# A gated cross-attention and mixture-of-experts layer on one core: SyncE's queue reordered, weights in two pairs of buffers, list scatters two per tile step, small tiles gathered four ahead

## The reference

```
x = x + tanh(g_xattn) * attention(layernorm(x), ctx, ctx)      # 16 heads of 16
x = x + tanh(g_ffn) * moe(layernorm(x))

def moe(xt):                                   # 4096 tokens, 8 experts, top 2
    logits = xt @ Wr + br
    gate = softmax of the two largest logits, 0 elsewhere
    h = relu(xt @ W1[e] + b1[e])               # 256 -> 1024, for each expert e
    y = h @ W2[e] + b2[e]                      # 1024 -> 256
    return sum over e of gate[e] * y
```

## Time and profile before

| | us |
|---|---|
| median of 3 runs | 882.1 (879.96 to 883.54) |
| profiled execution | 884.82 |
| its span, first to last instruction | 883.1 |
| PE busy | 753.8 |
| DVE busy | 612.7 |
| POOL busy | 438.3 |
| ACT busy | 407.7 |

### The profile page before, as it was taken

One profiled execution on the slowest core, in us unless ns is written; L12 is line 12 of the kernel. 1 busy time (PEld: TensorE's weight loads), 2 busy tenths in 40 slices (PEclk: granted clock), 3 DMA queues, 4 the chain that ended last, 5 costly groups with the idle time before them and its releaser, 6 DMA issues.

```text
span 883.1 us, 22095 instructions
## 1 busy us (share of the span) xinstructions
PE 753.8 (85%) x6602; PEld 503.6 (57%) x6603; DVE 612.7 (69%) x1279; ACT 407.7 (46%) x784; POOL 438.3 (50%) x439
## 2 busy tenths in 40 slices
PE   3489988888888989875799789999999999999765
PEld 2145555545555555432567567767777777776543
DVE  5567899999797989974457767666666666666333
ACT  2046767776676767755233223333333333333220
POOL 5112433555555565436654745555555555554322
PEclk9579999999999999987799999999999999999788
DMA  4334655666565656544312233222222232223111
GB/s 131 109 106 120 190 167 177 185 180 171 161 168 159 182 169 179 150 111 131 91 25 38 31 45 46 47 48 48 48 48 48 48 48 48 48 42 49 26 20 23
DMA packets 96292, 85.15 MB, mean 96 GB/s; under 512 B 21702, under 2 KB 85516, under 8 KB 96108
## 3 DMA queue, kind: packets, MB, share of 16 engines
q1 hardware_dynamic: 80268, 65.72, 26.6%
q0 software_dynamic: 15680, 18.69, 13.6%
q10 hardware_dynamic: 288, 0.00, 0.0%
HBM read 53.61 MB, written 30.62 MB: 95 GB/s over the span
## 4 chain that ended last, share of the span: by engine, by line
PE 29%; DMA 26%; DVE 18%; issue 16%; POOL 5%; ACT 3%; SPq 1%; DVEq 1%; POOLq 1%; ACTq 0%
DMA out_dram<-yb,dest_idx 20%; DVE negmax L1081 6%; PE banks L1756 5%; PE banks L1658 4%; PE banks L1577 3%; DMA xg<-xn_rows,gather_idx 3%; PE banks L1554 3%; PE banks L1742 2%; PE banks L1744 2%; PE banks L1743 2%; ACT probs L882 2%; PE banks L1646 2%; DVE stats L1005 2%; POOL xg L688 2%; PE banks L1625 2%
## 5 line engine op out<-in xcount | busy, mean ns | idle before, releaser
L954 ACT ACTIVATE hid<-banks,b_col 128x256 f32<-128x256 f32 (+1 forms) x312 | 124.1, 451 | 238.7 <-PE banks L1744 128.1
L1756 PE MATMUL banks<-wall,hh 128*128 x568 | 210.1, 389 | 4.3 <-DVE yb L1495 4.1
L745 POOL DMA_INDIRECT out_dram<-yb,dest_idx x71 | 123.7, 1743 | 169.0 <-DMA out_dram<-yb,dest_idx 81.2
L1742 PE MATMUL banks<-xh,wall 128*128 128x256 f16 (+1 forms) x624 | 167.9, 272 | 15.7 <-DVE xl L1432 14.4
L1081 DVE TENSOR_REDUCE negmax<-banks 128x4 f32<-128x1024 f32 x128 | 155.8, 1217 | 27.8 <-PE banks L1625 27.2
L1743 PE MATMUL banks<-xl,wall 128*128 128x256 f16 (+1 forms) x624 | 167.8, 272 | 0.0
L1744 PE MATMUL banks<-xh,wall 128*128 128x256 f16 (+1 forms) x624 | 167.7, 272 | 0.0
L882 ACT ACTIVATE probs<-banks 128x1024 f32<-128x1024 f32 x128 | 131.1, 1024 | 67.8 <-PE banks L1646 67.3
L1756 PE MATMUL banks<-wall,hl 128*128 x568 | 147.4, 279 | 0.0
L1658 PE MATMUL banks<-probs,vaug 128*32 128x256 f32 x1024 | 84.0, 400 | 28.0 <-ACT probs L882 17.5
L688 POOL DMA_INDIRECT xg<-xn_rows,gather_idx x71 | 86.9, 1224 | 37.7 <-issue 21.2
(11 more groups left out here) (206 smaller groups left out, 1201.7 us busy)
## 6 DMA issues: line engine op xcount, KB each, us to landing
wst<-in_L_ffn_W SPq DMA_DIRECT2D x30, 512.0 KB, 5.1
k_parts<-kparts SPq DMA_DIRECT2D x48, 128.0 KB, 3.4
ks<-k_parts SPq DMA_DIRECT2D x64, 96.0 KB, 2.2
q_parts<-qparts SPq DMA_DIRECT2D x48, 128.0 KB, 2.0
qs<-q_parts SPq DMA_DIRECT2D x64, 96.0 KB
xin<-in_x SPq DMA_DIRECT2D x16, 256.0 KB, 5.4
cin<-in_ctx SPq DMA_DIRECT2D x16, 256.0 KB, 6.9
xres<-in_x SPq DMA_DIRECT2D x16, 256.0 KB, 4.8
```

Source lines behind the costliest of these rows:

```text
L745: nc.gpsimd.indirect_dma_start(out_rows, bass.IndirectOffsetOnAxis(dest_idx[par][:, s:s + 1], 0), yb[par][:, s, :], None, compute_op=ALU.a ...
L954: ins = nc.scalar.activation(hid[half][:, c % (HC // 2), 0:subs(j) * P], banks[:, b, c % 2 * TS:c % 2 * TS + subs(j) * P], ACT.Relu, bias= ...
L1742: nc.tensor.matmul(dst, hi, xh[par][:, m, 0:rows], start=(m == 0), stop=False)
L1756: ins = nc.tensor.matmul(dst, h_[:, c, s * P:(s + 1) * P], w_, start=(c == 0 and k == 0), stop=(c == HC - 1 and k == 1))
```

## The change

- SP's queue: x and context are loaded three batches ahead, behind the loads of q's first half; the weights come first in a body; xres is issued one body earlier; the second halves of ks and qs are loaded at the end of the body before; output rows and normalized rows are issued apart. At the start both stores of parts precede all reloads, and x of batch 2 is loaded at once.
- Weight halves go by turns to raw and wst, four buffers; raw gets its own place in SBUF, and xh and xl lie over it. The late halves move forward by some places.
- PE computes k of batch 1 before the first scores. Tiles 0 and 1 are gathered at the end of POOL's body 15. After the last body, the turn of batch 15 stands first; the ranks of group 6 go to step 0, its places and entries to DVE's step 0.
- POOL sends groups 6 and 7 in steps 1 to 4 and 6 to 9, two sends each, behind the gather.
- Small tiles: each half of xg has its own semaphore and holds one tile; steps 30 and 31 gather two small tiles each, later ones tile j + 4. y of small tiles goes to banks 6 and 7 by turns, and DVE makes xl, and the first half of the hidden layer, before the result.
- 14 tile steps are written out at first, and the attention loop is one lap shorter.

```diff
+at["raw"] = A[0]
+raw = [sb(f"raw{i}", [P, M * H // 2], F32, A) for i in range(2)]
...
-LEAD, PEELED, TILE_LEAD = 4, 6, 8
+LEAD, PEELED, TILE_LEAD, TABLES_AT = 4, 6, 14, 7
...
+def half_of(j):
+    return (j - BIGS) // 2 % 2
+def y_bank(j, par, s):
+    return 6 + (s if subs(j) == SUB else par)
...
+stage = [raw[0], raw[1], wst[0], wst[1]] * 2
...
+arrival = [raw, wst]
...
+    load_x(2, 1, 0)
...
-        for h in range(2):
+    for h in range(2):
+        for name in "kq":
             load_part(0, 0, name, h)
...
+        if i < 4:
+            hold(sp, stage_free[i % 2], 2 * W_KEPT + i // 2)
+        elif i >= 4:
+            hold(sp, late_lo, i - 3)
...
-        if turns:
-            load_x(m + 2, t + 1, par)
-        if maxima and within(m, 1, NB):
-            load_part(m, par, "k", 1)
-            load_part(m, par, "q", 1)
         if attention:
             max_row(m - 1, 1 - par, 1)
-        if post:
-            residual(m - 2)
+        if weights:
+            for w in range(2):
+                e = t - 1
+                wait(sp, stage_free[w], 2 * (t - 1) + par)
...
+                sp.dma_start(stage_view(arrival[par][w], w), src).then_inc(w_full[par][w], 16)
+        if isinstance(m, int) and m == NB - 2:
+            late_load(0)
+            late_load(1)
         if isinstance(m, int) and m == NB - 1:
-            late_load(2)
...
+            late_load(4)
+            late_load(5)
...
-        if post:
-            results(m - 2)
-        if weights:
...
+        if within(m, 0, NB - 4):
+            load_x(m + 3, t, 1 - par)
...
-            late_load(4)
-            late_load(5)
+            hold(sp, table_ready, 2)
+            hold(sp, list_sent, 16 * 2 * PAIR * EARLY_PAIRS)
+            for j in range(2):
+                slot_load(j)
             late_load(6)
             late_load(7)
+        if post:
+            result_rows(m - 2)
+        if within(m, 1, NB):
+            residual(m - 1)
+        if ahead:
+            load_part(m + 1, 1 - par, "k", 1)
+            load_part(m + 1, 1 - par, "q", 1)
+        if isinstance(m, int) and m == NB:
+            for j in range(2, 6):
+                slot_load(j)
+        if post:
+            norm_rows(m - 2)
+        if isinstance(m, int) and m == NB - 2:
+            late_load(2)
+            late_load(3)
...
+    def gather_small(j, par):
+        h, turn = half_of(j), (j - BIGS) // 4
+        if turn == 0:
+            hold(pool, xg_full[par], 16 * SUB * (BIGS // 2))
+            hold(pool, gT_done, BIGS - 1 + par)
+        else:
+            hold(pool, xg_half[par][h], 16 * turn)
+            hold(pool, gT_done, j - 3)
+        hold(pool, slots_full[par], 16 * (j // 2 + 1))
...
+        nc.gpsimd.indirect_dma_start(xg[par][:, h, :], None, xn2_d,
+                                     bass.IndirectOffsetOnAxis(gather_idx[par][:, h:h + 1], 0)).then_inc(xg_half[par][h], 16)
...
-        last = isinstance(m, int) and m == NB
-        if last:
+        if sending and par == 0:
+            paced(3, 3)
+        if post:
+            norm2(m - 2)
+        if isinstance(m, int) and m == NB - 1:
             hold(pool, av_mm, 8 * (NB - 1))
             hold(pool, xn2_stored, 16 * EARLY_PAIRS * 2)
             gather(0, 0, 0)
-        elif sending and par == 0:
-            paced(3, 3)
-        if post:
-            norm2(m - 2)
-        if last:
             gather(1, 0, 1)
-            for n in range(3, 6):
-                send_entry(t - 3, n)
-        elif sending and par == 0:
+        if sending and par == 0:
             paced(4, 5)
...
     residual(NB - 1)
-    tokens(NB // 2 - 2)
     gather(2, 1, 0)
     norm2(NB - 1)
     gather(3, 1, 1)
-    enlist(NB // 2 - 2, 0)
-    enlist(NB // 2 - 2, 1)
-    tokens(NB // 2 - 1)
+    tokens(NB // 2 - 2)
...
+        fixed = isinstance(j, int)
+        if not fixed or 2 <= j < BIGS - 2:
             gather(j + 2, t + 1, i)
-        if there(j, -2) and subs(j - 2 if isinstance(j, int) else j) == SUB:
+        elif j >= BIGS - 2:
+            ahead = (2 * j - BIGS + 4, 2 * j - BIGS + 5) if j < BIGS else (j + 4,)
+            for x_ in ahead:
+                if x_ < NT:
+                    gather_small(x_, x_ % 2)
+        if fixed and 1 <= j < 5:
+            send_entry(NB // 2 - 2, 2 * (j - 1))
+            send_entry(NB // 2 - 2, 2 * (j - 1) + 1)
+        if fixed and j == 5:
+            tokens(NB // 2 - 1)
+        if fixed and 6 <= j < 10:
+            send_entry(NB // 2 - 1, 2 * (j - 6))
+            send_entry(NB // 2 - 1, 2 * (j - 6) + 1)
+        if fixed and j == EARLY - 3:
+            hold(pool, xn2_stored, 16 * NB)
+        if there(j, -2) and subs(j - 2 if fixed else j) == SUB:
             scatter(j - 2, i, 1, t - 1)
         if there(j, -1):
             scatter(j - 1, 1 - i, 0, t + (i - 1) // 2)
-        if isinstance(j, int) and j in (3, 4):
-            enlist(NB // 2 - 1, j - 3)
-        if isinstance(j, int) and j == TILE_LEAD - 1:
...
+        if isinstance(j, int) and j == 0:
+            act.wait_ge(late_lo, 5)
...
-        late_at_step = {NB - 1: {0: 0, 1: 1, 6: 2, 7: 3}, NB: {2: 4, 3: 5, 4: 6, 5: 7}}.get(m, {}) if isinstance(m, int) else {}
+        late_at_step = {NB - 1: {0: 0, 1: 1, 3: 2, 4: 3, 6: 4, 7: 5}, NB: {0: 6, 1: 7}}.get(m, {}) if isinstance(m, int) else {}
...
+                if isinstance(m, int) and m == NB:
+                    high_x(0, 0)
...
-        late_at_step = {NB - 1: {1: 0, 2: 1, 7: 2}, NB: {0: 3, 3: 4, 4: 5, 5: 6, 6: 7}}.get(m, {}) if isinstance(m, int) else {}
+        late_at_step = {NB - 1: {1: 0, 2: 1, 4: 2, 5: 3, 7: 4}, NB: {0: 5, 1: 6, 2: 7}}.get(m, {}) if isinstance(m, int) else {}
...
-            if isinstance(m, int) and m == NB - 1 and w == 6:
+            if isinstance(m, int) and m == NB - 1 and w == 3:
                 early_table()
...
     low_x(0, 0)
-    n, q = NB - 1, NB // 2 - 2
-    places(q)
-    router(n - 1, 0)
+    n = NB - 1
     attended(n, 0)
     attended(n, 1)
-    choose_place(q)
+    router(n - 1, 0, 7)
     attended_low(n)
     cut_hidden(0, 0, 0)
-    sum_place()
     residual(n)
     norm2_stats(n)
-    whole_place(q)
-    gate_sum(q)
-    gate_share()
-    gate_first(q)
-    gate_second()
-    carry_on(q)
     cut_hidden(0, 0, 1)
     low_x(1, 1)
...
+        after_small = fixed and j > BIGS
         if there(j, -1):
             e = dve.value_load(tile_expert[0:1, ds(j - 1, 1)], min_val=0, max_val=E - 1)
+        if there(j, -1) and not after_small:
             result(j - 1, t + (i - 1) // 2, 1 - i, 0, e)
         if there(j, 2):
             low_x(j + 2, i)
-        if fixed and j == 2:
-            places(q)
-            choose_place(q)
-            sum_place()
-            whole_place(q)
-            gate_sum(q)
+        if fixed and j in (0, 2):
+            places(NB // 2 - 2 + j // 2)
         if there(j, -1) and subs(j - 1 if fixed else j) == SUB:
             result(j - 1, t + (i - 1) // 2, 1 - i, 1, e)
-        if fixed and j == 2:
-            gate_share()
-            gate_first(q)
-            gate_second()
         if fixed and j == 3:
             share_out()
         if fixed and j == 4:
             later_table()
         if fixed and j == 5:
+            entries(NB // 2 - 1)
+        if fixed and j == 6:
             small_table()
-        if there(j, 1):
-            for half in range(2):
+        for half in range(2):
+            if there(j, 1):
                 cut_hidden(j + 1, 1 - i, half)
+            if half == 0 and after_small and there(j, -1):
+                result(j - 1, (j - 1) // 2, 1 - i, 0, e)
         if fixed and j == 0:
             router(NB - 1, 1, 7)
-            listed_top(q)
+            entries(NB // 2 - 2)
+            carry_on(NB // 2 - 2)
+            listed_top(NB // 2 - 1)
+        elif fixed and j == TABLES_AT:
+            dve.wait_ge(table_ready, 6)
         elif fixed and j == TILE_LEAD - 2:
             passed_rows()
...
     def gathered_T(j, lap, par):
-        pe.wait_ge(xg_full[par], 16 * subs_to(lap + 1))
+        if subs(j) == SUB:
+            pe.wait_ge(xg_full[par], 16 * subs_to(lap + 1))
+        else:
+            pe.wait_ge(xg_half[par][half_of(j)], 16 * ((j - BIGS) // 4 + 1))
...
             pe.wait_ge(hl_ready, 2 * (j + 1))
-            wait(pe, y_ready, slot_at(j - 1) + s + 1)
+            if subs(j) == SUB:
+                wait(pe, y_ready, slot_at(j - 1) + s + 1)
+            else:
+                pe.wait_ge(y_ready, slot_at(j - 2) + 1 if j - 2 >= BIGS else slot_at(BIGS - 1) + 1 + par)
...
-        mm = [(banks[:, 6 + s, 0:2 * D], hh[par], both), (banks[:, 6 + s, 0:D], hl[par], both[:, 0, :])]
+        at = y_bank(j, par, s)
...
+            first_batch = isinstance(m, int) and m == 0
+            if u == 0 and first_batch:
+                k(1, 1, 0)
+                k(1, 1, 1)
...
-    router(n - 1, NB // 2 - 2)
+    turn_out(n, 0)
+    turn_out(n, 1)
+    router(n - 1, None, 7)
...
     first(0, 0, e, 0)
     first(0, 0, e, 1)
-    turn_out(n, 0)
```

(19 more changed lines are left out.)

124 lines of the change are left out of this document (55 added, 69 removed).

## The result

| | before | after |
|---|---|---|
| median (runs) | 882.8 (4: 880.0 to 884.2) | 860.5 (4: 859.3 to 861.6) |
| profiled execution, span | 884.82, 883.1 | 861.55, 859.8 |
| ratio, 95% interval | | 0.9718 (0.9677 to 0.9759) |

The sign was right; the time was not: predicted were 840 us, in a range of 826 to 856. Of the 42 us forecast, 22 came by the medians and 23 by the spans of the two profiles; 19 to 20 are missing.

What follows compares the result with a forecast made beforehand. No engine full; stages bounded differently, the tile stage by POOL's ring of scatter landings and PE together. Terms -5 - 6 - 7 + 5 - 3 - 26 = -42 gave 842.8 us profiled, 840.1 on the median, taken as 840; range 826 to 856.

Steps and rivals of the forecast that it cites:

- Start, -5: Kernel start: stores before reloads move first scores by 2.9 us at most, k product of batch 1 saves 2.7; gain 5.
- Attention, -6: Attention batches: earlier xres ends POOL's wait, two disturbed batches gain 3 us each, other batches nothing; bounds 0 and 10.
- Change of stage, -7: Between attention and tiles: 8.8 us of three PE waits go, less added weight halves and ranks; gain 7, bounds 0 and 12.
- Lists, +5: Tile steps with two list sends: 16 us added to POOL's scatter ring, 11 us of old waits saved; costs 5.
- six steps written out, -3: Tile steps 8 to 13 lose the loop's register work: 3 us off, bounds 0 and -5.
- The loop, 0: Stretch from tile 14 to tile 31: no gain or loss predicted, 0.
- Small tiles, -26: From tile 28 on: only POOL's ring of scatter landings remains, 73.7 us instead of 99.7; PE's path 66; bounds 13 and 33.
- The first: Rival: small tiles stay slower, by landings of 4.4 us or DVE's result; seven tiles at 6.6 us, 853 us; chance 16%.
- The second: Rival: list sends cost more, gathers some 2 us late and the clock falls; 848 to 852 us; chance 10%.
- The fourth: Rival: slower than before, SP's early x load delays ks and qs halves in 13 batches; 892 at 4 us each; chance 4%.
- the fifth: Rival: gathers four tiles ahead still wait behind POOL's ring, tail as before; 866 us; chance 3%.
- The page on the time of a transfer: Skill page's DMA formula: 2.3 us landing for 128 KB, sends free, sum about -54; set aside for the trace's 3.78 to 4.35.

Runs made afterwards that it cites:

- the second profile: The changed kernel itself, unaltered, run and profiled again as yardstick of another set: 863.07 us, ratio 0.9789 to the kernel before.
- the kernel of 829.67 us: Changed kernel plus sends in the landing gap, small tiles' registers kept, new order at the change of stage, POOL's addition after DVE cuts cT: 829.67 us, ratio 0.9329.

## Why the prediction was wrong, point by point

- **Start, -5: right** (-5.6, and -4.8 in the second profile). The split is not confirmed: without the k product's move V of batch 0 comes 2.7 us later, as forecast, but V of batch 1 stands where it stands in other profiles.
- **Attention, -6: wrong** (-1.1 and +0.7; nothing between batches 5 and 14). The step that failed is "a transfer that lands sooner in them ends no wait", which took the other batches as they were. From batch 5 on POOL's wait for xres did go, and so did both waits for xn2b; but an addition that starts sooner stands beside other DVE instructions, and it holds some of them. The size is shown: 6.5 us between batches 5 and 14 came back without the addition, and 5.4 with the addition placed elsewhere. I had costed an instruction that moves only by its own time.
- **Weights, 0: nothing speaks against it.** No wait of PE or DVE names them in the loop; it wasn't tried by itself.
- **Change of stage, -7: half in one profile, whole in the other** (-3.6 and -7.0; the other profiles with this order give 2.2 to 6.8, and the kernel before, in the run with 14 steps written out, took 70.1 us here and not 65.4). Whatever the size, a part was missed. Of the three waits, those for the gather and the places went. The third, for xl, was a wait for DVE's order: the prediction ended at "takes the places and entries out from before the xl of tile 1" and didn't ask what stood there still: residual, statistics and the second cut.
- **Lists, +5, and six steps written out, -3: right.** Together +1.7 and +4.0 in the two profiles, where +2 was forecast, the steps alone -2.9 in the kernel before. Yet "the other seven add 7 x 2.58" is true only for sends ahead of the first scatter; in the landing gap between the two they cost nothing, and I had the idle 3 us before me in the earlier trace rows.
- **The loop, 0: +2.6 and +1.0, not clear of the spread.** POOL reached two gathers late (PE waited 1.31 us at 629 and 1.60 at 774). The kernel before has such waits too (1.37 us at 592, 1.32 at 736), and so has the kernel of 829.67 us, whose sends aren't late (1.39 at 604). Their cause is open.
- **Small tiles, -26: wrong** (-17.3). The ring was priced right: with the register loads out of the way it is 69.2 us from the first scatter of tile 28 to the last (784.18 to 853.41), where I had 69.2. What failed is "PE's own path is shorter: five of half (5.4)". A step of half the width isn't half the time, since the 1.27 us for two register loads don't shrink and come to light: 5.5 us became 6.9, and the scatters waited for DVE's result at that pace and not for a landing. That is 4.9 us (777.31 to 851.42 is 74.1, not 69.2). The other 3.9 are the drain, 8.4 us from last scatter to the end instead of the 4.5 read off. The -17.3 hang on the kernel before as well: with the 93.7 us that this stretch took in the run with 14 steps written out, they would be -12.8.
- **Rivals.** The first, small tiles at 6.6 us each, was what happened, by another cause than the two I named; alone it gave 853, and with 5 us of attention and 3.4 of the change of stage it is 861. I had let the rivals come one at a time. The second (sends at the upper end) didn't come as a time, though its sign did: PE waited 0.9 to 2.6 us for gathered rows in seven steps, as forecast, and those seven took 17 us more than quiet ones, under the 26 set as a limit. The fourth (SP's load of x holding the second halves) and the fifth didn't come: no wait of PE for ks or qs within a batch shows.
- **The page on the time of a transfer** gave 2.3 us for a landing. In the chains of waits of all 17 profiles no scatter landed in less than 3.56 us; about half took up to 3.9, and single ones up to 6.6.

## What to carry to other kernels

A transfer or an instruction that moves earlier meets new neighbours: look at what runs on VectorE beside a GpSimd instruction that reads two SBUF operands, and put it beside one that reads PSUM. On a queue whose bound is a ring of landings, whatever else it must issue belongs into the wait for a landing, not ahead of the transfer. And when the width of a step is halved, its fixed parts (register loads, waits for semaphores) are not: list them before dividing a step's time by two.

## What was not expected of the hardware

- POOL's closing DRAIN took two values and none between in 17 profiles: it ends 0.5 us after the last transfer landed, or some 4.3 us after it (4.2 or 8.1 us from that transfer's issue). With the change it was the longer in all 15 profiles; the cause is open.
- A DVE instruction of 0.16 us whose record starts 0.55 us before POOL's addition, and which should have been over by then, was held until that addition ended. The order of the records alone doesn't say who holds whom.
- PE's sequencer takes 0.3 us to load a register from SBUF and 0.15 us to work on it; in steps of 256 columns that is covered by products already queued, in steps of 128 it leaves PE idle for 0.97 us.
